# A two-layer decoder on one core: score products of 8 or 9 rows widened to the 32 rows of their band

## The chip, the cores and the metric

One core of one Trainium2 chip. The metric is the device time of one execution of the whole kernel, in microseconds; the kernel before has a median of 2346.39 us over 3 runs (2345.46 to 2348.4).

## What is computed

Two decoder layers over x (4 batches, 512 tokens, width 128), each of self attention, cross attention and a mixture of experts, each step followed by a layer norm. The change touches one piece, the self attention inside the first layer's feed-forward step. It has 16 heads of width 8 and no mask:

```python
def attention(x, w_qkv, b_qkv, w_o, b_o):
    qkv = x @ w_qkv + b_qkv
    q, k, v = jnp.split(qkv, 3, axis=-1)          # each to (B, T, 16, 8)
    scores = jnp.einsum('bqhd,bkhd->bhqk', q, k) / jnp.sqrt(jnp.float32(dh))
    probs = jax.nn.softmax(scores, axis=-1)
    ctx = jnp.einsum('bhqk,bkhd->bqhd', probs, v).reshape(B, T, D)
    return ctx @ w_o + b_o
h = x + attention(layer_norm(x, ln1_w, ln1_b), w_qkv, b_qkv, w_o, b_o)
```

## The kernel before

The program runs its stages one after the other, each in a block of its own: a causal self attention with bf16 parts stacked in 128 rows (`narrow_causal_attention`, lines from 828), a cross attention of the same kind with 96 rows (score products L1430), the full self attention of the change (`narrow_full_attention`, called with the tag "c"), the first experts (products L2497 and L2507), the second layer's self attention with heads of 64 rows (L1687), its cross attention, and the second experts.

In `narrow_full_attention` the work goes by groups of 4 heads of one batch: 4 batches times 4 groups are 16 groups (`STEPS`). A group has 16 items m (`TILES`): 4 tiles of 128 queries (or keys) times 4 heads. Everything is f32, and each f32 product stands in the trace as two matmul records.

- `queries(u)` and `keys(u)` (L564, L569): one product each of 128 rows with 512 columns makes q and k of a group, transposed. Their weights `WP` are padded: head j of the group lies in rows 32j to 32j+31 of the output (a band), the 8 numbers of the head first and the other 24 rows zero. ACT copies q into `QG` (L698), DVE k into `KG` (L773), with biases `BC` padded alike, so that all rows of a band are written. Row 8 of a band of `KG` is one (`BP[:, 1, :, HD8]`); row 8 of a band of `QG` is zero until SyncE writes the negated maxima into it (L513).
- `score(m)` (L587): scores with a row per query, for the maxima alone. The operands are the 8 rows of a band: `head(j, HD8)`. DVE takes the maximum of each row of 512 (L765). Three PSUM banks go round, so score m waits for maximum m-3.
- `turn_maxima(u)` (L593): the maxima of a group are turned by PE, copied by ACT (L713) and written by four DMAs into row 8 of the bands of `QG`.
- `score_by_key(m)` (L604): scores with a row per key, with 9 rows of a band, `head(j, HD8 + 1)`, so that the maxima are subtracted by the product itself. ACT takes the exponential (L707) out of one of three other PSUM banks.
- `value_products(w)` (L616): after four items, 4 products of 128 rows and 32 columns each, one for each head, which lie side by side in the array.
- `turn_heads` (L624), `normalise` (L789, L792) and, once for each batch, the output product and the residual with its norm.

The order on PE is written out by hand in `tensor`: 24 scores ahead (`MAXIMA_LEAD`), then for each item `score(m + 24)`, `score_by_key(m)` with the head two bands further on, after each fourth item the value products of the four before, and between them at fixed places the queries, keys, turns and outputs. Products in different bands run at the same time: two items in a row take all four bands.

The helper that cuts the bands, and the two calls that use it for scores:

```python
def head(j, rows):
    return slice(CW * j, CW * j + rows)      # CW = 32, HD8 = 8
```

Of the kernel before, what the change touches and what calls it, by code (L numbers as in the profile page):

```python
# [11 lines left out]
P = 128  # L12
# [7 lines left out]
HD8 = P // H  # L20
# [5 lines left out]
CW = P // GH  # L26
# [399 lines left out]
def narrow_full_attention(c, tag, weights, early=None):  # L426
# [11 lines left out]
    nc = c.nc  # L438
# [3 lines left out]
    MBANKS = [c.ps_s[:, i, :] for i in range(3)]  # L442
    KBANKS = [c.ps_s[:, 3, :], c.ps_t[:, 0, :], c.ps_t[:, 1, :]]
    PTS = 3
    with ExitStack() as own:
# [4 lines left out]
        QG = c.sb(f"{tag}_QG", [P, 3, S], F32, own)  # L450
        KG = c.sb(f"{tag}_KG", [P, 3, S], F32, own)
# [50 lines left out]
        def head(j, rows):  # L502
            return slice(CW * j, CW * j + rows)

        with nc.Block() as block:
# [40 lines left out]
            def _(pe):  # L546
# [32 lines left out]
                def score(m):  # L579
                    u, i = divmod(m, TILES)  # L580
                    qt, j = divmod(i, GH)
                    if i == 0:
                        pe.wait_ge(s_qout, u + 1)
                        pe.wait_ge(s_kout, u + 1)
                    if m >= 3:
                        pe.wait_ge(s_max, m - 2)
                    nc.tensor.matmul(MBANKS[m % 3], QG[head(j, HD8), u % 3, qt * P:(qt + 1) * P], KG[head(j, HD8), u % 3, :],  # L587
                                     start=True, stop=True).then_inc(s_m, 1)

                def turn_maxima(u):  # L590
# [5 lines left out]
                def score_by_key(m):  # L596
                    t, i = divmod(m, TILES)
                    kt, j = divmod(i, GH)
                    j = (j + 2) % GH
                    if i == 0:  # L600
                        pe.wait_ge(s_row, rows_all * (t + 1))
                    if m >= 3:
                        pe.wait_ge(s_exp, m - 2)
                    nc.tensor.matmul(KBANKS[m % 3], KG[head(j, HD8 + 1), t % 3, kt * P:(kt + 1) * P],  # L604
                                     QG[head(j, HD8 + 1), t % 3, :], start=True, stop=True).then_inc(s_st, 1)

                def value_products(w):
                    t, kt = divmod(w, QT)
# [48 lines left out]
                for m in range(MAXIMA_LEAD):  # L657
                    score(m)
                turn_maxima(0)
                for m in range(ALL):  # L660
                    t, i = divmod(m, TILES)
                    b, g = divmod(t, GROUPS)
                    if m + MAXIMA_LEAD < ALL:
                        score(m + MAXIMA_LEAD)
                    score_by_key(m)
                    if i % GH == GH - 1 and m >= TILES // 2 - 1:
                        w = m // GH - 1
                        value_products(w)
                    if i == 0 and t + 2 < STEPS:
                        queries(t + 2)  # L670
                    if i == 4 and t + 2 < STEPS:
                        keys(t + 2)
                    if i == 7 and t:
                        turn_heads(t - 1)
                    if i == 9 and t + 1 < STEPS:
                        turn_maxima(t + 1)
                    if i == 13:
                        if g == 0 and b + 1 < B:
                            values(b + 1)
                        if g == 1 and b:  # L680
                            turn_context(b - 1)
                        if g == 2 and b:
                            output(b - 1)
                        if g == 3 and b:
                            back(b - 1)
# [1982 lines left out]
```

## Time and profile before

| | |
|---|---|
| median of 3 runs | 2346.39 us |
| profiled execution, its own time | 2343.91 us |
| its span, first to last instruction | 2342.2 us |
| PE busy (matmul) | 2015.3 us, 86% |
| PE weight load busy | 1033.7 us, 44% |
| DVE busy | 1270.1 us, 54% |
| ACT busy | 1020.0 us, 44% |
| GpSimd busy | 143.0 us, 6% |
| mean granted TensorE clock | 0.816 of full speed |

Busy time of PE counts every stretch in which a matmul is under way, also where four small ones run side by side. The granted clock is the share of full speed that the chip gives to TensorE; 1.00 is 2.4 GHz and 0.50 is 1.2 GHz. The stage of the change runs from about 545 to 1150 us of the span.

### The profile page before, as it was taken

The numbers are of one execution on the slowest core, as the hardware profiler recorded it, in microseconds if no ns is written. First come the engines' busy times: TensorE is split into PE (matmuls) and PEld (weight loads), VectorE is DVE, ScalarE is ACT, GpSimd is POOL, SyncE is SP. The second block draws the span as 40 slices with busy tenths as digits, with TensorE's granted clock in tenths as the row PEclk, the third lists the DMA queues.
The fourth block names the chain that finished last, engine by engine and source line by source line (L and its number), as shares of the span: only waits on it lengthen the run. The fifth ranks groups of instructions, "written<-read, shape, count | busy, mean of one in ns | idle before, by whom it ended". The sixth has DMA issues, their size and how long they took to land. (4 is left out here: it accounts for less than half of the span.)

```text
span 2342.2 us, 31089 instructions
## 1 busy us (share of the span) xinstructions
PE 2015.3 (86%) x9958; PEld 1033.7 (44%) x9958; DVE 1270.1 (54%) x3981; ACT 1020.0 (44%) x2074; POOL 143.0 (6%) x228
## 2 busy tenths in 40 slices
PE   3288874865999999999799977999999998998997
PEld 2144442543322222222377753445454545665664
DVE  7398875645433333333233337776766673674445
ACT  3288871650232232233243425776767673332221
POOL 2000000003000000000000001000000000330000
PEclk7599995985555555555599987999999999898999
DMA  2533202400000000000100011000000000000000
GB/s 57 79 45 37 23 0 46 60 15 0 1 1 1 1 1 0 1 1 1 28 19 19 18 36 37 1 1 1 1 1 1 1 1 1 2 1 18 17 20 25
DMA packets 46252, 36.27 MB, mean 15 GB/s; under 512 B 11732, under 2 KB 42681, under 8 KB 46137
## 3 DMA queue, kind: packets, MB, share of 16 engines
q1 hardware_dynamic: 46137, 34.80, 8.4%
q8 instruction: 65, 1.06, 0.2%
q14 instruction: 50, 0.41, 0.1%
HBM read 28.86 MB, written 5.77 MB: 15 GB/s over the span
## 5 line engine op out<-in xcount | busy, mean ns | idle before, releaser
L765 DVE TENSOR_REDUCE c_NM<-ps_s 128x1 f32<-128x512 f32 x256 | 169.6, 687 | 327.3 <-PE ps_s L587 327.3
L587 PE MATMUL ps_s<-c_KG,c_QG 8*128 8x512 f32 x512 | 307.5, 1092 | 0.8 <-DVE c_NM L765 0.8
L604 PE MATMUL ps_t<-c_QG,c_KG 9*128 9x512 f32 x340 | 269.7, 1092 | 1.3 <-ACT c_PT L707 1.3
L707 ACT ACTIVATE c_PT<-ps_t 128x512 f32<-128x512 f32 x170 | 99.8, 596 | 247.7 <-PE ps_t L604 151.0
L1771 ACT ACTIVATE d_PR<-d_PR,d_NM 128x512 f32<-128x512 f32 x256 | 183.8, 718 | 32.8 <-DVE d_NM L1842 32.8
L1780 ACT ACTIVATE d_PT<-ps_t 128x512 f32<-128x512 f32 x256 | 150.5, 589 | 105.7 <-PE ps_t L1696 105.7
L2582 DVE SCALAR_TENSOR_TENSOR X<-ps_t,GATE,X 128x128 f32<-128x128 f32 x272 | 76.7, 344 | 184.5 <-PE ps_t L2507 184.4
L604 PE MATMUL ps_s<-c_QG,c_KG 9*128 9x512 f32 x172 | 171.0, 1093 | 2.6 <-DMA c_QG<-c_NMT 2.0
L1842 DVE CUSTOM_DVE_ANT_0 d_PR<-ps_s,d_BH 128x512 f32<-128x512 f32 x256 | 165.4, 684 | 0.3 <-PE ps_s L1687 0.2
L993 ACT ACTIVATE a_PR<-a_PR,a_NM 128x128 f32<-128x128 f32 (+3 forms) x256 | 129.8, 555 | 79.0 <-DVE a_NM L974 79.0
L903 PE MATMUL ps_t<-ident,a_PR 128*128 128x128 f32 x640 | 115.4, 289 | 47.1 <-ACT a_PT L917 38.1
L587 PEld LDWEIGHTS ps_s<-c_KG,c_QG 8*128 8x128 f32 x512 | 91.2, 303 | 140.6 <-issue 91.3
L1687 PE MATMUL ps_s<-d_K,d_Q 64*128 64x512 f32 x512 | 145.0, 644 | 1.3 <-DVE d_NM L1842 1.3
L1696 PEld LDWEIGHTS ps_t<-ident,d_PR 128*128 128x128 f32 x1024 | 117.0, 141 | 61.1 <-issue 32.5
L2544 ACT ACTIVATE f_HT<-ps_s,f_BE 128x512 f32<-128x512 f32 x128 | 87.8, 687 | 128.7 <-PE ps_s L2497 128.0
L1696 PE MATMUL ps_t<-ident,d_PR 128*128 128x128 f32 x1024 | 135.4, 275 | 4.4 <-DVE d_PR L1852 4.3
L1709 PE MATMUL ps_v<-d_PT,d_VB 128*64 128x512 f32 x512 | 137.4, 617 | 0.9 <-DVE d_CT L1860 0.9
L2497 PE MATMUL ps_s<-XT,g_W 128*128 128x512 f32 x288 | 132.0, 602 | 1.6 <-DVE g_HT L2561 1.6
L2507 PEld LDWEIGHTS ps_t<-f_W,f_HT 128*128 128x128 f32 x1024 | 119.2, 192 | 14.8 <-issue 14.3
L616 PE MATMUL ps_v<-c_PT,c_VG 128*32 128x512 f32 x512 | 123.5, 1059 | 0.0
L2507 PE MATMUL ps_t<-f_W,f_HT 128*128 128x128 f32 x1024 | 119.3, 275 | 0.0
L2497 PE MATMUL ps_s<-XT,f_W 128*128 128x512 f32 x256 | 117.7, 604 | 0.3 <-DMA f_W<-in_L_ffn_w 0.3
(339 smaller groups left out, 3251.1 us busy)
## 6 DMA issues: line engine op xcount, KB each, us to landing
QX<-split_parts SPq DMA_DIRECT2D x72, 128.0 KB
KX<-split_parts SPq DMA_DIRECT2D x36, 128.0 KB
f_W<-in_L_ffn_w SPq DMA_DIRECT2D x16, 256.0 KB, 3.1
split_parts<-a_PARTS SPq DMA_DIRECT2D x8, 384.0 KB, 11.0
g_W<-in_L_ffn_w SPq DMA_DIRECT2D x24, 128.0 KB, 2.2
split_parts<-b_PARTS SPq DMA_DIRECT2D x4, 384.0 KB, 10.3
X<-in_x SPq DMA_DIRECT2D x4, 256.0 KB
c_QG<-c_NMT SPq DMA_DIRECT2D x64, 2.0 KB
```

The lines of the kernel that those rows point to most:

```text
L587: nc.tensor.matmul(MBANKS[m % 3], QG[head(j, HD8), u % 3, qt * P:(qt + 1) * P], KG[head(j, HD8), u % 3, :], start=True, stop=True).then_in ...
L604: nc.tensor.matmul(KBANKS[m % 3], KG[head(j, HD8 + 1), t % 3, kt * P:(kt + 1) * P], QG[head(j, HD8 + 1), t % 3, :], start=True, stop=True) ...
L765: nc.vector.tensor_reduce(NM[:, u % 2, j, qt:qt + 1], MBANKS[m % 3], AX.X, ALU.max, negate=True).then_inc(s_max, 1)
L993: nc.scalar.activation(PR[:, j % 2, qt, 0:k], PR[:, j % 2, qt, 0:k], ACT.Exp, bias=NM[:, j % 2, qt:qt + 1]).then_inc(exped, 1)
L1687: mm = nc.tensor.matmul(c.ps_s[:, 2 * (n % 2) + e, :], Q[half(e), g % 2, qt * P:(qt + 1) * P], K[half(e), g % 2, :], start=True, stop=True)
L1696: mm = nc.tensor.transpose(c.ps_t[:, e, kt * P:(kt + 1) * P], PR[:, n % RING, e, kt * P:(kt + 1) * P], c.ident[:, :])
L1709: mm = nc.tensor.matmul(c.ps_v[half(e), :], VB[:, g % 2, kt, half(e)], PT[:, g % 2, e, kt, :], start=(kt == 0), stop=(kt == QT - 1))
L1771: nc.scalar.activation(PR[:, n % RING, e, :], PR[:, n % RING, e, :], ACT.Exp, scale=-1.0, bias=NM[:, n % RING, e:e + 1], accum_out=DEN[:, ...
L1780: nc.scalar.activation(PT[:, g % 2, e, :, qt * P:(qt + 1) * P], c.ps_t[:, e, :].rearrange("p (k q) -> p k q", q=P), ACT.Copy).then_inc(tak ...
L1842: nc.vector.tensor_tensor_reduce(out=PR[:, n % RING, e, :], in0=c.ps_s[:, 2 * (n % 2) + e, :], in1=BH[:, 2 * p + e, S - P - qt * P:2 * S - ...
L2497: nc.tensor.matmul(c.ps_s[:, ch, :], W[:, (ch % CH) * P:(ch % CH + 1) * P], c.XT[:, b * S:(b + 1) * S], start=True, stop=True).then_inc(s_ ...
L2507: mm = nc.tensor.matmul(c.ps_t[:, b % 2, q * P:(q + 1) * P], HT[:, b % 2, ch, q * P:(q + 1) * P], W2[i][:, ch, :], start=(ch == 0), stop=( ...
```

## The change

Both kinds of score products take all 32 rows of the band in place of 8 and 9. No instruction is added, removed or moved, on any engine; only the row count in the operands of the products L587 and L604 differs. The further rows hold zeros in both operands, but for row 8, which in `score(m)` is one in `KG` and still zero in `QG`, as the maxima are written there only after the last score of the group.

```diff
-                    nc.tensor.matmul(MBANKS[m % 3], QG[head(j, HD8), u % 3, qt * P:(qt + 1) * P], KG[head(j, HD8), u % 3, :],
+                    nc.tensor.matmul(MBANKS[m % 3], QG[head(j, CW), u % 3, qt * P:(qt + 1) * P], KG[head(j, CW), u % 3, :],
                                      start=True, stop=True).then_inc(s_m, 1)
...
-                    nc.tensor.matmul(KBANKS[m % 3], KG[head(j, HD8 + 1), t % 3, kt * P:(kt + 1) * P],
-                                     QG[head(j, HD8 + 1), t % 3, :], start=True, stop=True).then_inc(s_st, 1)
+                    nc.tensor.matmul(KBANKS[m % 3], KG[head(j, CW), t % 3, kt * P:(kt + 1) * P],
+                                     QG[head(j, CW), t % 3, :], start=True, stop=True).then_inc(s_st, 1)
```

## Rows read from the trace of the kernel before

**Rows 1.** The page: busy tenths of the span in 40 slices

```profile
PE   3288874865999999999799977999999998998997
PEclk7599995985555555555599987999999999898999
```

**Rows 2.** Busy time by stretch: causal, cross, lead, main part, second layer

```profile
core 0: us, PE busy (x) PEld busy (x) DVE busy (x) ACT busy (x) POOL busy (x), PEclk, DMA share, GB/s
120.00:335.00 215.00, 173.19 (x1299) 94.09 (x1295) 191.01 (x1094) 182.39 (x410) 11.34 (x56) 1.00 0.26 28
432.00:480.00 48.00, 40.03 (x360) 26.06 (x364) 32.49 (x82) 33.70 (x74) 1.50 (x8) 1.00 0.37 50
577.00:604.00 27.00, 24.70 (x51) 11.35 (x51) 16.68 (x26) 0.27 (x1) 0.00 (x0) 0.50 0.00 1
630.00:1110.00 480.00, 462.48 (x1530) 128.16 (x1533) 167.63 (x299) 145.46 (x273) 9.09 (x11) 0.52 0.00 1
...
1460.00:1940.00 480.00, 474.52 (x2490) 235.79 (x2490) 334.28 (x972) 322.30 (x751) 3.81 (x6) 1.00 0.00 1
```

**Rows 3.** Groups by line, 604 to 1141 us: busy us, mean ns | idle before, releaser

```profile
L587 PE MATMUL ps_s<-c_KG,c_QG 8*128 8x512 f32 x462 | 282.9, 1087 | 0.0
L604 PE MATMUL ps_t<-c_QG,c_KG 9*128 9x512 f32 x340 | 269.7, 1092 | 1.3 <-ACT c_PT L707 1.3
L765 DVE TENSOR_REDUCE c_NM<-ps_s 128x1 f32<-128x512 f32 x231 | 153.6, 687 | 317.8 <-PE ps_s L587 317.8
L564 PE MATMUL ps_f<-XT,c_WP 128*128 128x512 f32 x28 | 29.1, 1142 | 0.0
```

**Rows 4.** Timeline of PE, part of a group: start, us, instructions [idle before <-releaser]

```profile
800.84 1.22 PE L587 MATMUL ps_s<-c_KG,c_QG 8*128 8x512 f32 x1
...
802.86 1.94 PE L616 MATMUL ps_v<-c_PT,c_VG 128*32 128x512 f32 x8
804.73 1.22 PE L587 MATMUL ps_s<-c_KG,c_QG 8*128 8x512 f32 x1
...
806.73 2.08 PE L564 MATMUL ps_f<-XT,c_WP 128*128 128x512 f32 x2
808.74 1.22 PE L587 MATMUL ps_s<-c_KG,c_QG 8*128 8x512 f32 x1
...
812.45 1.94 PE L616 MATMUL ps_v<-c_PT,c_VG 128*32 128x512 f32 x8
...
828.39 0.37 PE L593 MATMUL ps_f<-ident,c_NM 128*16 128x128 f32 x1 [1.34 <-DVE CTX L792]
```

**Rows 5.** Timeline around 720 to 728 us

```profile
720.36 1.94 PE L616 MATMUL ps_v<-c_PT,c_VG 128*32 128x512 f32 x8
722.23 1.12 PE L624 MATMUL ps_f<-ident,c_CT 128*128 128x128 f32 x4
...
726.04 0.27 PE L593 MATMUL ps_f<-ident,c_NM 128*16 128x128 f32 x1 [1.36 <-DVE CTX L792]
726.24 0.69 PE L587 MATMUL ps_s<-c_KG,c_QG 8*128 8x512 f32 x1
...
727.31 1.94 PE L616 MATMUL ps_v<-c_PT,c_VG 128*32 128x512 f32 x8
727.40 1.29 DVE L765 TENSOR_REDUCE c_NM<-ps_s 128x1 f32<-128x512 f32 x2 [0.91 <-PE ps_s L587]
```

**Rows 6.** Busy time by stretch: in the first, second and last spell, and after the second

```profile
656.00:657.00 1.00, 0.86 (x8) 0.03 (x4) 0.12 (x1) 0.08 (x1) 0.00 (x0) 1.00 0.00 0
...
724.00:725.00 1.00, 0.69 (x8) 0.00 (x0) 0.28 (x1) 0.24 (x1) 0.00 (x0) 1.00 0.00 0
728.00:730.00 2.00, 2.00 (x12) 0.52 (x8) 0.69 (x2) 0.67 (x3) 0.00 (x0) 0.50 0.00 1
...
1141.00:1142.00 1.00, 0.47 (x4) 0.42 (x4) 0.00 (x0) 0.48 (x1) 0.00 (x0) 1.00 0.00 0
```

**Rows 7.** Busy time by stretch, one turn of maxima to the next

```profile
794.85:828.69 33.84, 32.50 (x109) 8.43 (x109) 11.46 (x20) 10.60 (x20) 0.00 (x0) 0.51 0.00 1
```

## The prediction

> **What bounds the kernel now.** I read the page's slices first [rows 1]. In slices 9 to 19, some 640 us, PE is busy nearly all the time and yet has half the clock: the only long stretch of the kernel in which it works steadily at 1.2 GHz. That is the stage of the change. Next the busy times by stretch [rows 2]: from 630 to 1110 us PE is busy 462 of 480 us at a granted clock of 0.52, with DVE at 168 us and ACT at 145 us. The groups by line [rows 3] say who waits: DVE's maxima sat idle 317.8 us for the score products, and those products have next to no idle time ahead of them. So PE bounds the stage, and it runs at half speed. The timeline [rows 4] then gives the price of each step at that clock, and a short spell at full clock [rows 5, 6] gives the same steps at 2.4 GHz.
>
> **What the change removes and adds.** It removes nothing. If the chip took the products with 32 rows as it took those with 8 and 9, the kernel would stay as it is. Direct cost first. A product of 9 rows takes as long as one of 8, 1092 against 1087 ns, and one of 128 rows 1142 ns [rows 3]. The last is nearly four times as many rows as 32, and most of its 50 ns go with its having the array to itself. I take zero; the ends are 0 and 50 ns a record. The products still stay inside their bands, so two items side by side still take all four. Queues, DMAs and waits are untouched.
>
> **Why the clock should move.** The question is what keeps this stage at 0.50, and the stretches answer it by comparison [rows 2]. The first self attention has the full clock while PE is busy 173 of 215 us, the cross attention while it is busy 40 of 48. The stage of the change has half the clock while PE is busy 96% of the time. So it isn't a lack of busy time. What differs is how much of the array a product uses: 128 rows in the first, 96 and 128 in the second, 64 rows and more in the second layer's attention (1460 to 1940 us), all at 1.00; here four products side by side use 32 to 36 rows of 128.
>
> Inside the stage the clock rose six times for a few microseconds each [rows 6] (the first, the second and the last of them stand there), and it is always the same place: value products directly followed by more work on the whole array (five times the head turns L624, once, at the end, a second set of value products). At 720.36 come eight value records, at 722.23 four turns, and at 724 the clock is 1.00 [rows 5, 6]. Then come the scores of 8 and 9 rows and the 1.36 us wait at the turn of the maxima, and it falls again [rows 5, 6]. Value products with 32 columns each count when four of them lie side by side, so products side by side add up, and four of 32 rows should add up to the whole array as well.
>
> Do zeros count as work? The head turns multiply by an identity matrix, nearly all zeros, and they belong to the work before the rises. The causal stage has 56 zero rows in its 128 [rows 2]. Both say that the rows named in the instruction count, not what is in them.
>
> The Trainium skill speaks against the change here ("TensorE: Matmul & The Clock Gate", Part 1): the gate follows how busy PE has been. By that rule rows of zeros change nothing and the time would stay at 2346; the trace disagrees, with 0.50 at 96% busy beside 1.00 at 81%. The Trainium skill ("TensorE: Matmul & The Clock Gate", Part 4) also says that turns don't count as busy in the same way; the rise right behind the four turns at 722.23 speaks against that as well.
>
> With 32 rows an item pair fills the array as its value products do, so a group has hardly a stretch of small work left, and I expect the clock to rise soon after the first score by key (604 us), at about 612 us, and to stay. Before that, from 577 to 604 us, the 24 scores run alone in three bands at most with DVE between, and I leave them at 0.50.
>
> **The sum.** One group at half clock, in steps from the timeline [rows 4]:
> - two items side by side 800.84 to 802.86, 2.02 us, four times: 8.1;
> - one item alone (before queries and keys) 804.73 to 806.73, 2.00 us, twice: 4.0;
> - three items 808.74 to 812.45, 3.71 us, twice: 7.4;
> - value products 802.86 to 804.73, 1.87 us, four times: 7.5;
> - queries and keys, 806.73 to 808.74, 2.01 us each: 4.0;
> - head turns 1.1 us [rows 5], the turn of the maxima 0.3, the work once a batch about 1.0.
> Together 33.4 us, and 1.34 us of waiting for DVE ahead of the turn of the maxima (828.39): 34.7 us. (The measured turn-to-turn stretch in rows 7 is 33.8 us; it began inside a spell at full clock.)
>
> At full clock two items side by side took 726.24 to 727.31, 1.07 us [rows 5]: 0.53 of 2.02. The PE part becomes 33.4 x 0.53 = 17.7 us. The wait before the turn of the maxima was 1.36 us in the full-clock spell, as at half clock [rows 4, 5]: 19.0 us.
>
> What is late next? Each bank goes from PE to DVE and back: issue to maximum begun 1.14 us (726.26, the later of the two items, to 727.40), the maximum 0.69 us (two in 1.29), and some 0.1 us to the next product: about 1.9 us a round for three banks. PE alone needs 1.97 us for three items (3.71 x 0.53), and between most blocks come value products, queries or turns, in which DVE catches up. Only the last pair of a group follows so closely that it waits, 0.2 us by walking through the group: 19.2 us. DVE has 11.5 us of work in a group and ACT 10.6 [rows 7]; both fit. The ends of this term: nothing, or one maximum of 0.65 us bare in each of the eight blocks, 5.2 us.
>
> So a group goes from 34.7 to 19.2 us, 15.5 less, or 44.7% of the time. From 612 to 1141 us there are 529 us: 236 us. The six spells have had about 1.5 us each already: 9 off. Gain 227 us. The profiled execution took 2343.91 us, 2.5 below the median; it would become 2117, and the median 2346.4 - 227 = 2119 us. After 1141 us nothing changes but the moment at which the experts start against the chip's clock, a few microseconds either way.
>
> **Bounds.** Lower end: PE times exactly halved, no bank waits, the rise at 604: 16.7 + 1.34 = 18.0 us a group, 48% of 537 us less 9, 249 us; and if the lead of 24 scores also gets the full clock, with DVE's busy 16.7 of the 27 us [rows 2] as its limit, up to 8 us more. That is 2090. Upper end: the 5.2 us of bare maxima, 24.4 us a group, 157 less 9 = 148 us: 2198. I take 2092 to 2182, as the blocks leave DVE time to catch up.
>
> **The rivals.**
> - *The clock doesn't move* (chance 0.08): the chip counts bands in use, or zeros don't count. For it: a band is the unit by which the products are placed. Against: all four bands were in use before as well, at 0.50, and the turns with their identity. The time is 2346. The Trainium skill ("TensorE: Matmul & The Clock Gate", Part 3) has masks of 32-row strips in the instruction; if those were counted, 8 and 32 rows would be one, and the time 2346 as well.
> - *The clock swings* (0.06): PE twice as fast leaves gaps, at the turn of the maxima above all, and falls back there; all five spells in the middle of the stage ended around that wait [rows 5, 6]. If half of each group is at 1.2 GHz, half of the gain is left, 114 us: 2232. Against: in those spells the work on both sides of the wait had 8 and 9 rows, and the cross attention holds 1.00 with PE idle a sixth of the time [rows 2].
> - *Slower* (0.04): the clock stays at 0.50, and 32 rows take what 128 take, 50 ns a record more [rows 3]. 1024 score records, two to four at a time, are 256 to 512 steps: 13 to 26 us, about 2366. It decides if the mean of L587 rises above some 1.10 us with the clock unchanged.
>
> **How the numbers follow.** The forecast has 0.82, and its own range, 2092 to 2182, holds nearly all of it; the swinging clock is mostly above it. A measurement of this kernel tells about 0.2% (5 us) from no change. Faster 0.82 + 0.06 = 0.88, same 0.08, slower 0.04.
>
> **What would show it.** A granted clock of 1.00 in the page's slices from about 612 us; score records of some 0.6 to 0.7 us in place of 1.09; turns of the maxima 19 us apart; DVE's idle time for L587 down from 318 to some 100 us; stages before 577 us and the durations after the stage unchanged. If the clock stays at 0.50, the reading of the stretches is wrong; if it is 1.00 and groups take over 22 us, the bank round was undersized.

## The result, and the profile after

The changed kernel has a median of 2121.53 us over 4 runs (2119.73 to 2123.56), the kernel before beside it 2345.93 us. The ratio is 0.9044, with a 95% interval of 0.9029 to 0.9060: 224 us less. The forecast was 2119 us, faster, with a range of 2092 to 2182. Medians and ranges are of all executions of a kernel; the ratios with an interval leave out executions that are over 1.5% above the fastest of their kernel.

The page of the changed kernel, busy tenths in 40 slices, against [rows 1]; a slice is now 53 us:

```profile
PE   4177777486599899979999499999999989979997
...
PEclk7599998598579999989999699999999998999999
```

The clock reads 5 in the eleventh slice and 7 in the twelfth, where the stage begins, and 9 in the five after it, where it read 5 to the end of the stage. Busy time by stretch, with the columns of [rows 2]: the causal attention, the cross attention, the lead of 24 scores, the main part of the stage, and the second layer's attention.

```profile
120.00:335.00 215.00, 169.71 (x1274) 94.12 (x1294) 191.31 (x1099) 181.82 (x409) 11.35 (x56) 1.00 0.24 28
432.00:480.00 48.00, 39.78 (x335) 25.73 (x333) 30.60 (x76) 32.08 (x69) 1.32 (x7) 0.93 0.37 47
577.00:604.00 27.00, 24.24 (x53) 11.06 (x53) 17.11 (x26) 0.27 (x1) 0.00 (x0) 0.56 0.00 1
630.00:880.00 250.00, 226.74 (x1368) 70.44 (x1366) 149.72 (x267) 125.83 (x242) 7.60 (x8) 1.00 0.01 1
...
1230.00:1710.00 480.00, 475.40 (x2487) 235.75 (x2486) 335.31 (x977) 324.13 (x755) 3.81 (x6) 1.00 0.00 1
```

In the main part the granted clock is 1.00 throughout, where it was 0.52. The lead stays near 0.50 (0.56, with one spell). The stretches before and after the stage are what they were, but for one dip of the clock in the cross attention (0.93). The rise is here:

```profile
604.00:608.00 4.00, 4.00 (x8) 0.99 (x11) 0.00 (x0) 0.60 (x1) 0.00 (x0) 0.50 0.00 0
608.00:612.00 4.00, 4.00 (x17) 1.28 (x14) 2.31 (x4) 2.29 (x5) 0.00 (x0) 0.82 0.00 0
```

The groups by line, 612 to 911 us, against [rows 3]:

```profile
L587 PE MATMUL ps_s<-c_KG,c_QG 32*128 32x512 f32 x454 | 157.1, 632 | 0.0
L765 DVE TENSOR_REDUCE c_NM<-ps_s 128x1 f32<-128x512 f32 x228 | 149.8, 686 | 109.3 <-PE ps_s L587 109.2
...
L616 PE MATMUL ps_v<-c_PT,c_VG 128*32 128x512 f32 x492 | 65.6, 604 | 5.8 <-ACT c_CT L719 5.8
...
L587 PEld LDWEIGHTS ps_s<-c_KG,c_QG 32*128 32x128 f32 x454 | 48.0, 183 | 67.4 <-DVE c_NM L765 59.4 <-issue 5.4
L604 PEld LDWEIGHTS ps_t<-c_QG,c_KG 32*128 32x128 f32 x330 | 42.7, 183 | 15.7 <-issue 9.6 <-ACT c_PT L707 5.8
```

A score record takes 632 ns in place of 1087. DVE's idle time for the scores is 109 us, not 318. The weight loads of the score products now wait 59 us for DVE's maxima, but PE itself is never idle ahead of those products (0.0). In the timeline of PE the steps of [rows 4] stand at 2.4 GHz, among them the wait ahead of the turn of the maxima, unchanged at 1.34 us, and a new one of 0.44 us:

```profile
700.18 1.16 PE L575 MATMUL ps_f<-c_W,XT 128*128 128x128 f32 x8
...
702.34 1.06 PE L616 MATMUL ps_v<-c_PT,c_VG 128*32 128x512 f32 x8
703.33 0.69 PE L587 MATMUL ps_s<-c_KG,c_QG 32*128 32x512 f32 x1
...
704.39 1.13 PE L564 MATMUL ps_f<-XT,c_WP 128*128 128x512 f32 x2
705.44 0.69 PE L587 MATMUL ps_s<-c_KG,c_QG 32*128 32x512 f32 x1
...
707.36 1.06 PE L616 MATMUL ps_v<-c_PT,c_VG 128*32 128x512 f32 x8
...
712.90 1.07 PE L616 MATMUL ps_v<-c_PT,c_VG 128*32 128x512 f32 x8 [0.44 <-ACT c_CT L719]
...
716.97 0.27 PE L593 MATMUL ps_f<-ident,c_NM 128*16 128x128 f32 x1 [1.34 <-DVE CTX L792]
...
720.31 0.66 PE L631 MATMUL ps_f<-ident,CTX 128*128 128x128 f32 x4
...
836.93 0.27 PE L593 MATMUL ps_f<-ident,c_NM 128*16 128x128 f32 x1 [1.34 <-DVE CTX L792]
```

### The profile page after: what moved, and what is told of

It reads as the page before. It is cut to its first block and busy times, and to the rows that moved or that the text cites. A ratio compares the mean times of both kernels' runs of the same rounds, so it can differ in the third digit from the quotient of the medians.

```text
span 2118.3 us, 31066 instructions
## 1 busy us (share of the span) xinstructions
PE 1782.2 (84%) x9935; PEld 982.5 (46%) x9958; DVE 1268.8 (60%) x3981; ACT 1016.8 (48%) x2074; POOL 143.0 (7%) x228
## 5 line engine op out<-in xcount | busy, mean ns | idle before, releaser
L587 PE MATMUL ps_s<-c_KG,c_QG 32*128 32x512 f32 x512 | 184.4, 677 | 0.8 <-DVE c_NM L765 0.8
L604 PE MATMUL ps_t<-c_QG,c_KG 32*128 32x512 f32 x340 | 151.3, 637 | 1.3 <-ACT c_PT L707 1.3
L1852 DVE TENSOR_SCALAR d_PR<-d_PR,d_RDEN 128x512 f32<-128x512 f32 x256 | 113.0, 484 | 4.6
L903 PEld LDWEIGHTS ps_t<-ident,a_PR 128*128 128x128 f32 x640 | 70.8, 142 | 96.1 <-ACT a_PT L917 47.9
L2542 ACT ACTIVATE g_GT<-ps_s 128x512 f32<-128x512 f32 x72 | 43.0, 598 | 141.8 <-PE ps_s L2497 141.8
```

Of the source, the lines that this page charges most:

```text
L587: nc.tensor.matmul(MBANKS[m % 3], QG[head(j, CW), u % 3, qt * P:(qt + 1) * P], KG[head(j, CW), u % 3, :], start=True, stop=True).then_inc( ...
L604: nc.tensor.matmul(KBANKS[m % 3], KG[head(j, CW), t % 3, kt * P:(kt + 1) * P], QG[head(j, CW), t % 3, :], start=True, stop=True).then_inc( ...
L903: last = nc.tensor.transpose(c.ps_t[:, qt % 2, kt * P:(kt + 1) * P], PR[:, j % 2, qt, kt * P:(kt + 1) * P], c.ident[:, :])
```

## The experiments

The theory to be tested, theory A: the clock follows how much of the array the products use, rows times columns, added up over those that run side by side, and rows of zeros count. Its rivals: a product counts as a whole band from some row count on (B), the data count, or the rows help without the clock (C).

**How many rows.** Both products with 16, 20 and 24 rows:

```diff
-                    nc.tensor.matmul(MBANKS[m % 3], QG[head(j, CW), u % 3, qt * P:(qt + 1) * P], KG[head(j, CW), u % 3, :],
+                    nc.tensor.matmul(MBANKS[m % 3], QG[head(j, 16), u % 3, qt * P:(qt + 1) * P], KG[head(j, 16), u % 3, :],
...
-                    nc.tensor.matmul(KBANKS[m % 3], KG[head(j, CW), t % 3, kt * P:(kt + 1) * P],
-                                     QG[head(j, CW), t % 3, :], start=True, stop=True).then_inc(s_st, 1)
+                    nc.tensor.matmul(KBANKS[m % 3], KG[head(j, 16), t % 3, kt * P:(kt + 1) * P],
+                                     QG[head(j, 16), t % 3, :], start=True, stop=True).then_inc(s_st, 1)
```

> Both score products take 16 rows in place of 32. Theory A (what sets the clock is how much of the array, rows times columns summed over products side by side, is at work): the clock rises more often than with 8 and 9 rows and still falls at the places with little work, so it swings, about a third of the stage at 2.4 GHz, some 2270 us, between the two kernels. Theory B (a product counts as a whole band from some row count on): either 2346 or 2121 us, nothing between. Theory C (32 rows help in another way than by the clock): a time between with a clock that stays at 0.50.

> 20 rows in both score products, turn of the maxima where the change has it. Between 16 rows (2346) and 24 rows (2142 us). Theory A, by degrees: the clock swings, 2180 to 2330 us with a wide spread between executions. A step at one row count: 2346 or 2142 us.

> Both score products take 24 rows. Theory A: the work around the turn of the maxima is then large enough that the clock doesn't fall once it is up, and it rises within some tens of microseconds of 604 us: 2121 to 2135 us, granted clock 1.00 in the main part of the stage. Theory B: 2346 or 2121 us. If zeros had a cost of their own, it would be a little faster than with 32 rows.

Measured, medians with the spread of the runs:

| rows in both score products | time, us | clock in the main part |
|---|---|---|
| 8 and 9 (before) | 2346 (2343 to 2348) | 0.52 |
| 16 | 2346 (2342 to 2351), ratio 0.9996 (0.9987 to 1.0006) | 0.51 |
| 20 | 2243 (2227 to 2309), ratio 0.954 (0.9499 to 0.9582) | 0.72 |
| 24 | 2142 (2132 to 2157), ratio 0.9151 (0.9115 to 0.9187) | 0.97 |
| 32 (the change) | 2122 (2120 to 2124) | 1.00 |

The main part of the stage with 16, 24 and 20 rows, in the profile of each kernel:

```profile
630.00:1110.00 480.00, 462.49 (x1527) 127.64 (x1520) 165.90 (x290) 145.06 (x272) 7.61 (x8) 0.51 0.00 1
```

```profile
630.00:880.00 250.00, 227.79 (x1332) 69.50 (x1328) 146.32 (x261) 123.23 (x237) 7.60 (x8) 0.97 0.01 1
```

```profile
630.00:950.00 320.00, 300.31 (x1318) 87.02 (x1319) 144.93 (x258) 122.09 (x232) 7.58 (x8) 0.72 0.00 1
```

Nothing but a row count differs, and with 16 rows PE's busy time (462.49 us) is that of the kernel before to a hundredth. The time goes with the clock in all three. With 20 rows it lies halfway, with a spread of 82 us, because the clock is up in some stretches and down in others. That excludes a step at one row count (B) and a help without the clock (C). My expectation for 16 rows, 2270 us, was a miss: I had the rises last, but in its profile each of the few rises was lost again at once. That for 24 rows, 2121 to 2135 us and a clock of 1.00, was a small one: in its profile the clock dips four times for some microseconds, at about 676, 737, 799 and 860 us, each time right behind a turn of the maxima (674.95, 736.38, 798.08 and 859.54). With 32 rows there are no dips.

**One kind of product only.** 32 rows in the maxima's products with 9 left in those by key, and 32 by key with 8 left for the maxima:

```diff
-                    nc.tensor.matmul(KBANKS[m % 3], KG[head(j, CW), t % 3, kt * P:(kt + 1) * P],
-                                     QG[head(j, CW), t % 3, :], start=True, stop=True).then_inc(s_st, 1)
+                    nc.tensor.matmul(KBANKS[m % 3], KG[head(j, HD8 + 1), t % 3, kt * P:(kt + 1) * P],
+                                     QG[head(j, HD8 + 1), t % 3, :], start=True, stop=True).then_inc(s_st, 1)
```

> Only the products for the maxima take 32 rows, those by key keep 9. Theory A: half of the added work, so the clock swings, about 60% of the stage high, some 2210 us (range 2130 to 2290). Theory B with each product judged by itself: half of the products count, which gives a clock either up or down throughout, 2121 or 2346 us. The last 24 items, where no maxima are left, fall back to 0.50 by theory A.

> Only the products by key take 32 rows, those for the maxima keep 8. Theory A: as with the maxima alone, the clock swings, some 2215 us (range 2130 to 2290); the first 24 scores are at 0.50 throughout, as before. Theory B: 2121 or 2346 us.

Measured: 2252 us (2178 to 2295) and 2276 us (2231 to 2337), without an interval, since single executions differ by over 100 us. The difference arises in the stage: from the experts' first product (L2359) to the end the profiled execution of 2295 us takes 1187.8 us, that of the kernel before 1187.2. Both medians lie between the ends, as 20 rows do, and in the range expected, though above the 2210 and 2215 us named. Either half of the change alone leaves the clock swinging. Where does it fall? The timeline of PE with the maxima's products alone, at the end of a stretch of 30 us at full clock:

```profile
669.64 0.59 PE L587 MATMUL ps_s<-c_KG,c_QG 32*128 32x512 f32 x1
...
671.60 0.27 PE L593 MATMUL ps_f<-ident,c_NM 128*16 128x128 f32 x1 [1.34 <-DVE CTX L792]
671.79 1.21 PE L587 MATMUL ps_s<-c_KG,c_QG 32*128 32x512 f32 x1
671.80 1.21 PE L604 MATMUL ps_s<-c_QG,c_KG 9*128 9x512 f32 x1
```

The records before the turn of the maxima last 0.59 us, those right after it 1.21: the clock went down at PE's wait for DVE. Up to the last turn of the maxima every fall in the profiles of these two kernels stands within 3 us behind such a turn.

**Without that wait.** The turn of the maxima after item 11 of a group, its copy right after exponential 11:

```diff
-                    if i == 9 and t + 1 < STEPS:
+                    if i == 11 and t + 1 < STEPS:
                         turn_maxima(t + 1)
...
-                    if i == 10 and t + 1 < STEPS:
+                    if i == 11 and t + 1 < STEPS:
                         maxima_out(t + 1)
```

This was done with 32 rows for the maxima alone, with 16 rows in both, and with the 8 and 9 rows of the kernel before.

> 32 rows for the maxima alone, as in that experiment (2252 us), and the turn of the maxima after item 11. Theory A says the clock swings there because it falls at the stretch with little work, and that stretch is the wait ahead of the turn: without the wait it should stay up far longer, 2130 to 2190 us. If the falls have nothing to do with the wait, the time moves by the wait alone, 2252 less some 15, with the same spread.

> 16 rows in both score products, which gave 2346 us with a few spells at full clock that all ended at the turn of the maxima, and the turn after item 11. Theory A: the stretch with the least work is gone, so that a spell that begins lasts; the time depends on how soon one begins, 2130 to 2320 us with a wide spread. If 16 rows are too few to hold the clock in any case: 2331 us.

> The kernel before (8 and 9 rows) with the turn of the maxima after item 11. The wait of 1.34 us in 13 groups goes: some 15 us less at half clock, about 2331 us. Theory A says that the scores themselves are too little work here, so a spell at full clock still ends at once or nearly so and the clock stays at 0.50 for nearly all of the stage. If the wait alone had held the clock down, the time would fall far below 2300.

| rows, maxima and by key | turn after item 9 | turn after item 11 |
|---|---|---|
| 8 and 9 | 2346 | 2344 (2339 to 2348), ratio 0.9991 (0.9965 to 1.0017) |
| 16 and 16 | 2346 (2342 to 2351) | 2241 (2225 to 2300), ratio 0.9531 (0.9491 to 0.9571) |
| 32 and 9 | 2252 (2178 to 2295) | 2144 (2131 to 2195), ratio 0.9106 (0.9081 to 0.9131) |
| 32 and 32 | 2122 | 2112 (see below) |

By the medians the same edit is worth nothing that can be told with 8 and 9 rows, 105 us with 16, about 108 us with 32 and 9, where the executions before and after it overlap, and about 10 us with 32. With 16 rows, in one profile, by stretch:

```profile
630.00:860.00 230.00, 230.00 (x721) 64.58 (x722) 80.72 (x140) 69.59 (x127) 3.48 (x4) 0.50 0.00 1
865.00:995.00 130.00, 127.33 (x745) 41.06 (x744) 79.58 (x143) 69.61 (x132) 3.80 (x4) 1.00 0.01 1
```

The clock rises late, after 860 us, and then holds to the end of the scores for the maxima, where with the wait it never held. Why it rises just then isn't shown. With 8 and 9 rows there was no wait either, and yet the clock stayed down:

```profile
630.00:1110.00 480.00, 478.65 (x1542) 136.20 (x1545) 167.74 (x302) 150.01 (x276) 10.11 (x11) 0.51 0.00 1
```

PE was busy 478.65 of 480 us at a clock of 0.51, and the three rises in this profile (at 688, 859 and 996 us) were lost within 5 us, with no wait near them. So two things are needed for the clock to hold, each shown by itself: enough rows in the score products, and no stretch in which PE has too little to do.

The run with 8 and 9 rows should have gained 15 us by the wait itself, and its median gained none (its interval allows 8 us). At half clock its timeline of PE has four items in a row where there were two, the wait and two more:

```profile
824.00 1.22 PE L587 MATMUL ps_s<-c_KG,c_QG 8*128 8x512 f32 x1
...
826.73 1.34 PE L587 MATMUL ps_s<-c_KG,c_QG 8*128 8x512 f32 x2
...
828.86 1.94 PE L616 MATMUL ps_v<-c_PT,c_VG 128*32 128x512 f32 x8
830.73 0.38 PE L593 MATMUL ps_f<-ident,c_NM 128*16 128x128 f32 x1
```

Four items in a row take 4.86 us (824.00 to 828.86), against twice 2.02 in [rows 4]: the fourth needs the bank of the first, and its weight load waits 0.64 us for DVE's maximum there. That gives back 0.8 us of each 1.34. The other 0.5 can be seen: twelve groups from turn to turn take 406.8 us (661.55 to 1068.32), where they took 413.0 (658.21 to 1071.21). The profiled execution has a span 4.6 us shorter, within the spread of the runs.

**Do zeros count?** The weights and biases of queries and keys multiplied by zero as they are padded. This kernel leaves out the attention's real scores: of the score operands only the row of ones in the keys isn't zero.

```diff
-                    nc.vector.tensor_copy(WP[:, w, :, 0:HD8], weights.W[:, w, :].rearrange("p (h d) -> p h d", d=HD8))\
+                    nc.vector.tensor_scalar(WP[:, w, :, 0:HD8], weights.W[:, w, :].rearrange("p (h d) -> p h d", d=HD8), 0.0, None,
+                                            ALU.mult)\
...
```

> As the changed kernel, but the padded weights and biases of queries and keys are multiplied by zero, so that all rows of the score operands hold zeros (but for the row of ones in the keys) and the softmax is uniform; instructions and shapes are the same. Theory A (the rows named count, not what is in them): the clock is 1.00 from about 610 us and the time 2121 us. Rival (the chip counts switching data, and the 8 real rows carried it): the clock is lower in the stage, up to the 2346 us of the kernel before.

Measured: 2124 us (2119 to 2135), ratio 0.9046 (0.9005 to 0.9087). Its main part:

```profile
630.00:880.00 250.00, 226.74 (x1369) 70.70 (x1367) 149.79 (x267) 125.86 (x242) 7.59 (x8) 1.00 0.01 1
```

The same PE busy time and clock as with real data. What the rows of the score products hold plays no part.

**A faster version.** The two waits that the changed kernel still shows, at the turn of the maxima and at the copy of the heads, taken out one after the other; the second edit is

```diff
-                    if i == 5 and t:
+                    if i == 4 and t:
                         heads_out(t - 1)
```

> The changed kernel once more, for comparison on the same chip as the next three: 2121 us.

> 32 rows as in the change, and the turn of the maxima stands after item 11 of a group in place of item 9, its copy on ACT right after exponential 11. PE waits 1.34 us there in 13 groups of the changed kernel, for DVE's normalisation. If that wait is real time of PE: 12 to 17 us less, 2105 to 2109 us. If the row of maxima then comes too late for the next group (five items of about 1 us against the copy and four DMAs), a wait of up to 2 us a group takes its place and the time is 2110 to 2135 us.

> As the one before, and ACT copies the heads out after exponential 4 in place of 5. The value products waited 0.44 us a group for that copy (5.8 us in all): 3 to 6 us below the one before, about 2101 us; no difference if the wait moves to the keys or the banks of the exponentials.

Measured beside one another: the changed kernel 2126 us (2115 to 2132), ratio 0.9043 (0.9020 to 0.9066) to the kernel before; with the turn after item 11 2112 us, 0.8998 (0.8978 to 0.9018); with the heads after exponential 4 as well 2106 us (2105 to 2109), 0.8969 (0.8953 to 0.8984). Main part of the last one:

```profile
630.00:880.00 250.00, 249.04 (x1448) 79.59 (x1447) 156.79 (x281) 136.64 (x259) 7.59 (x8) 1.00 0.01 1
```

PE is busy 249 of 250 us where it was busy 227. It beats both kernels: 242 us below the one before and 16 to 20 us below the changed one. By the medians the first edit gave 9 to 13 us rather than 12 to 17. By the traces it is 7: twelve groups take 232.5 us in place of 239.4, 0.6 less each and not 1.34, again because four items in a row cost more; they take 2.96 us (713.67 to 716.63), where two and two took 2.2. The second edit takes another 0.5 us off each group, as expected.

## Why the prediction was right

- **What the clock follows.** Right in direction and in the part that decides: rows count, whatever they hold, and not PE's busy time. 16, 20, 24 and 32 rows and the run with zeros show it. The prediction's own ground for zeros was thin: the products with 56 zero rows (as the kernel has them; [rows 2] doesn't show it) are 228 of some 1300 records of the causal stage, and it took the run with zeros to settle it. What wasn't tested is columns: no run changed them alone, so "rows times columns" is shown for rows only. Nor do the runs tell the rows of the stationary operand from those of the moving one, as they are the same number.
- **When it rises and whether it holds.** I said about 612 us, then to stay: it was up within 608 to 612 us, some 3 us sooner, and stayed to the end of the stage. The lead stayed low but for one spell, as assumed.
- **No cost of 32 rows.** Right. At half clock the first records after a change of operands take 1.22 us with 8 rows [rows 4] as with 32 (607.64 us in the changed kernel's timeline):

```profile
607.64 1.22 PE L587 MATMUL ps_s<-c_KG,c_QG 32*128 32x512 f32 x1
```

- **The group at full clock.** 19.2 us was forecast. In the changed kernel's timeline turns of maxima begin at 716.97 and, six groups later, at 836.93 us: 20.0 us each. Two terms were too small. The wait of 0.44 us for the copy of the heads wasn't in the sum at all. And the work once a batch (L575, L631, L638, L646), put at about 1.0 us a group at half clock and so 0.5 at full, is one piece in nearly every group, of 1.1 and 0.6 us in turn (700.18 and 720.31 us above), which makes 0.3 more. The bank round, 0.2 us in the sum, can't be much more: PE's idle time in twelve groups is 21.5 of 239.4 us, which is the waits of 1.34 and 0.44 us and nothing ahead of a score product. The weight loads of L587 wait 59 us for DVE in the main part (38 us before), but PE works off earlier products meanwhile.
- **What made up for it.** The group at half clock was too small in the sum as well, since there the same pieces take 2.0 and 1.05 us: the turns at 828.39 and 898.97 us, two groups without a spell, are 35.3 us apart each, not 34.7. So a group lost 15.3 us where 15.5 was forecast, and the total is off by only 3 (227 against 224 us). The factor of 0.53 was right: 2.02 became 1.07 us. That the miss is so small is partly luck: a wait that the sum didn't have stands against work at half clock that it had too low.
- **The rivals.** "The clock doesn't move" and "slower" didn't happen. "The clock swings" named the right place, the wait at the turn of the maxima, but for too few rows: in the profiles the clock passes that wait every time with 32, falls there at some turns with 24, 20 or one kind of product, and never passes it with 16.
- **The rule that spoke against it.** The Trainium skill ("TensorE: Matmul & The Clock Gate", Part 1), by which the clock follows how busy PE has been, doesn't give these results: with 16 rows PE was as busy as before, with 32 less busy (226.74 of 250 us), and only the latter had the full clock; with 8 and 9 rows and no wait PE was busy 478.65 of 480 us at 0.51.

## What to carry to other kernels

If PE is busy nearly all the time in a stage and the granted clock there is 0.50, look at the rows of its matmuls, not only for idle time (columns weren't tried): here products of few rows could be widened over rows that already held zeros at no cost in time, and it was worth 224 of 2346 us. A partial widening can give nothing, or a kernel whose time differs by 100 us between executions. Then look for the place at which PE has least to do, since a wait of 1.3 us in each of 13 groups cost 105 us with 16 rows, and about 10 us with 32.

## What the runs showed that I had not expected

- 16 rows, twice those of the kernel before, gave exactly nothing (0.9996), while 20 gave 100 us. The gain doesn't grow with the rows in proportion.
- The worth of one wait depends on the clock around it: 1.34 us in 13 groups were worth nothing that the medians show at half clock, 105 and about 108 us where the clock hung on it, and about 10 us at full clock.
- The causal attention, which nothing here touches, loses the full clock now and then. In another profile of the changed kernel its stretch reads 0.96 where it was 1.00, and that execution was 7 us longer in span (2125.0 against 2118.3), all of it ahead of the stage: its first turn of the maxima begins at 606.0 us in place of 599.3:

```profile
120.00:335.00 215.00, 175.15 (x1258) 93.96 (x1255) 184.26 (x1056) 175.04 (x393) 11.32 (x56) 0.96 0.25 28
```

- The data of the score products has no effect on the time that can be told: all zeros and real values agree within the interval.
